# Moving part of the delta net's first head into the stage before it, in a two-layer network on one core

## What is computed

```python
x = x + latent_cross_attention(norm(x), ctx)    # 16 heads, rotary
x = x + attention(norm(x))                      # 16 heads of 16, scores multiplied by a triangle
x = x + hadamard_ffn(norm(x))                   # 256 -> 2*1024 -> 256
x = x + cross_attention(norm(x), ctx)           # 16 heads of 16, causal
x = x + gated_delta_net(norm(x))                # 32 value heads of 128, 16 key heads of 128
x = x + mixture_of_experts(norm(x))             # 32 experts of 96, the best 8
```

```python
q, k, v = silu(conv4(h @ Wqkv.T))               # a causal convolution of 4 taps along the tokens
g = -exp(A_log) * softplus(h @ Wa.T + dt_bias);  beta = sigmoid(h @ Wb.T)
# per token:  state = state * exp(g);  delta = (v - k @ state) * beta
#             state = state + outer(k, delta);  out = q @ state
o = out * rsqrt(mean(out**2)) * norm_w * silu(h @ Wz.T);   y = o @ W_out.T
```

## Time and profile before

| | us |
|---|---|
| median of 3 executions | 1669.58 (1667.72 to 1670.84) |
| the profiled execution, its own time | 1666.14 |
| its span, from first to last instruction | 1664.3 |
| PE busy in the span | 1547.2 (93%) |
| DVE busy | 1130.2 (68%) |
| ACT, POOL busy | 598.3 (36%), 553.9 (33%) |

### The profile page before, as it was taken

The page is one execution under the profiler, slowest core; times in us unless marked ns, Lnnn a source line. Parts: engine busy times, 40 slices in busy tenths (PEclk is TensorE's granted clock), DMA queues, the critical chain, the costliest instruction groups (busy, mean ns, idle before and its releaser), DMA issues. The chain is left out here.

```text
span 1664.3 us, 34006 instructions
## 1 busy us (share of the span) xinstructions
PE 1547.2 (93%) x14224; PEld 1084.9 (65%) x14224; DVE 1130.2 (68%) x1745; ACT 598.3 (36%) x1038; POOL 553.9 (33%) x885
## 2 busy tenths in 40 slices
PE   7999679979996698999999999999999996999999
PEld 3444358867883366777777777767777784565556
DVE  4666487597675677788888888887788833543433
ACT  2223144345333334444444444444544531111110
POOL 1200052123211545556545465454564431000000
PEclk9999889989998799999999999999999997999999
DMA  7533300010000121121121221112211113200000
GB/s 217 159 90 91 76 1 1 25 28 1 1 1 7 30 42 35 42 56 47 37 52 42 47 50 48 37 46 43 55 46 34 43 27 151 84 1 0 13 1 13
DMA packets 150536, 75.76 MB, mean 46 GB/s; under 512 B 128304, under 2 KB 131632, under 8 KB 148592
## 3 DMA queue, kind: packets, MB, share of 16 engines
q1 hardware_dynamic: 150384, 73.60, 17.5%
HBM read 55.73 MB, written 17.83 MB: 44 GB/s over the span
## 5 line engine op out<-in xcount | busy, mean ns | idle before, releaser
L1719 DVE SCALAR_TENSOR_TENSOR acc<-PS,wc,acc 128x504 f32<-128x504 f32 (+2 forms) x384 | 281.4, 733 | 93.2 <-ACT acc L1452 84.1
L2004 PE MATMUL PS<-HT,wgu 128*128 128x512 f32 x384 | 173.8, 597 | 0.6 <-ACT HT L2050 0.6
L1452 ACT ACTIVATE acc<-PS,wc 128x512 f32<-128x512 f32 x128 | 87.8, 686 | 172.3 <-PE PS L1183 119.7
L1183 PE MATMUL PS<-HT,wv 128*128 128x512 f32 x256 | 128.6, 626 | 11.4 <-DVE acc L1719 11.4
L1729 DVE SCALAR_TENSOR_TENSOR y<-th,acc 128x512 f32<-128x512 f32 x128 | 115.9, 906 | 22.7 <-ACT th L1456 21.4
L1183 PE MATMUL PS<-HT,wkq 128*128 128x512 f32 x256 | 124.5, 610 | 6.6 <-DVE acc L1719 4.7
L1642 POOL TENSOR_TENSOR rr<-nm,con 128x16 f32<-128x16 f32 x16 | 46.8, 2927 | 241.1 <-DVE nm L1747 241.1
L1200 PE MATMUL PS<-wz,HT 128*128 128x256 f32 x512 | 125.1, 392 | 0.7 <-DMA wz<-in_gdn_w 0.7
L2004 PEld LDWEIGHTS PS<-HT,wgu 128*128 128x128 f32 x384 | 73.3, 192 | 74.8 <-issue 72.7
L2140 DVE SCALAR_TENSOR_TENSOR act<-th,PS 128x512 f32<-128x512 f32 x48 | 33.0, 687 | 127.2 <-ACT th L2064 127.2
L1346 PE MATMUL PS<-wo,ogT 128*128 128x256 f32 x512 | 115.3, 383 | 3.5 <-DVE dl L1782 2.4
(11 more groups left out here) (252 smaller groups left out, 3036.5 us busy)
## 6 DMA issues: line engine op xcount, KB each, us to landing
a_rows<-AT SPq DMA_DIRECT2D x16, 512.0 KB, 2.6
wk<-in_l0x_k SPq DMA_DIRECT2D x16, 384.0 KB, 3.6
wgu<-in_moe_gu SPq DMA_DIRECT2D x6, 1024.0 KB, 14.9
queries_scratch<-tts SPq DMA_DIRECT2D x32, 128.0 KB, 2.7
wkq<-in_gdn_w SPq DMA_DIRECT2D x16, 256.0 KB, 2.7
wv<-in_gdn_w SPq DMA_DIRECT2D x16, 256.0 KB, 2.7
wz<-in_gdn_w SPq DMA_DIRECT2D x16, 256.0 KB, 3.3
wo<-in_gdn_w SPq DMA_DIRECT2D x16, 256.0 KB, 3.0
```

The lines of the kernel that those rows point to most:

```text
L1183: mm = pe.matmul(PS[:, QB[q], :], w[:, o:o + DK], HT[:, k, f * 512:(f + 1) * 512], start=(k == 0), stop=(k == DC - 1))
L1452: a.activation(acc[:, f, :], PS[:, QB[q], :], ACT.Copy, scale=wc[:, h % 2, 4 * c + 3:4 * c + 4]).then_inc(s["tap"], 1)
L1719: v.scalar_tensor_tensor(a0, p0, wc[:, h % 2, 4 * c + 2 - k:4 * c + 3 - k], a0, ALU.mult, ALU.add).then_inc(s["conv"], 1)
L2004: mm = pe.matmul(PS[:, 2 * (i % 2) + w, :], wgu[:, m, k, w, :], HT[:, k, f * N:(f + 1) * N], start=(k == 0), stop=(k == DC - 1))
```

## The change

Four parts; all arithmetic on the values stays, but for its order.

1. *Stage two.* The four lists are written anew: the same units in another order, and new ones at the end, `w_project`, `w_tap`, `w_conv`, `w_tanh`, `w_silu` (units 0, 2 and 4 of head 0, all on tiles 0 to 3) and `w_ab` (the decay projections of tiles 0 to 6). Their buffers acc, th and half of y (yA) now lie over kvT and W2, which stage two has done with; yB is the other half.
2. *Start of stage three.* The order of head 0's other units is 1, 3, 5, 6, 7 (PLACE numbers them behind the three done). `project_ab` has one tile left and comes first; part of the elementwise work goes from DVE to POOL. All four z projections of head 0 stand ahead of `cross(0, 4)`, in banks 5 and 7. POOL does `substitute(1)` ahead of `clear(0)`.
3. *Every head.* `factors` takes the power of the k half first, and of the q half behind Et.
4. *End of stage three.* The mean square is taken ahead of the two `gate`s; the last scaling is split over POOL (first value head) and DVE (second), as are the two copies; the layer norm of tiles 0 to 3 is done between the two last residuals; the first four packs of expert weights (wg0) are loaded behind `blocks_in(0)`.

```diff
@@ stage two: starts of PE's and DVE's lists
-                turn_x(0, 0); turn_x(0, 1); context(0); turn_x(1, 0); out_x(0); score_x(2, 1); turn_x(1, 1); score_x(3, 1)
-                context(1); turn_x(2, 0); out_x(1); turn(0, 0); turn_x(2, 1); project(0, 0); context(2); turn(1, 0)
+                turn_x(0, 0); turn_x(1, 0); turn_x(0, 1); turn_x(1, 1); context(0); context(1); out_x(0); out_x(1)
+                score_x(2, 1); score_x(3, 1); turn_x(2, 0); turn(0, 0); project(0, 0); turn(1, 0); turn_x(2, 1); turn_x(3, 0)
...
-                spread_x(1, 0); spread_x(0, 0); sums_x(1, 0); sums_x(0, 0); spread_x(0, 1); butterfly(0); sums_x(0, 1)
-                butterfly(1); spread_x(1, 1); butterfly(2); sums_x(1, 1); spread_x(2, 0); residual(0, 0); spread_x(3, 0)
+                spread_x(1, 0); spread_x(0, 0); sums_x(1, 0); sums_x(0, 0); spread_x(0, 1); spread_x(1, 1); sums_x(0, 1)
+                sums_x(1, 1); butterfly(0); butterfly(1); butterfly(2); spread_x(2, 0); spread_x(3, 0); residual(0, 0)
@@ stage two: ends of the lists of PE, ACT and DVE
+                project(5, 1); down(6); down(7); scores(5, 1); turn(6, 2); turn_p(4, 1); project(6, 1); values(4, 1)
+                turn(7, 2); scores(6, 1); project(7, 1); project_out(4, 1); turn_p(5, 1); scores(7, 1); values(5, 1)
+                project_out(5, 1); turn_p(6, 1); values(6, 1); turn(4, 3); project_out(6, 1); w_project(0); turn(5, 3)
+                w_project(1); turn_p(7, 1); w_project(2); values(7, 1); turn(6, 3); project_out(7, 1); w_ab(); turn(7, 3)
...
+                keep_o(6, 1); keep_hT(4, 3); w_tap(0); keep_hT(5, 3); w_tap(1); keep_p(7, 1); w_tanh(0); keep_o(7, 1)
+                w_tanh(1); keep_hT(6, 3); w_tap(2); w_tanh(2); keep_hT(7, 3)
...
+                stats(5, 3); sums(7, 1); apply(5, 3); residual(6, 3); stats(6, 3); w_conv(0); apply(6, 3); w_conv(1)
+                w_silu(0); w_silu(1); residual(7, 3); w_conv(2); stats(7, 3); w_silu(2); apply(7, 3)
@@ stage two: the new units
+                def w_project(k):
+                    if k == 0:
+                        pe.wait_ge(s["hT0"], 8)
+                    elif k == 2:
+                        pe.wait_ge(s["w_conv"], 3)
+                    w = wk if k < 2 else wv
+                    for c in range(DC):
+                        o = c * 2 * DK + (k % 2) * DK
+                        mm = pe.matmul(PS[:, k % 2, :], w[:, o:o + DK], HT[:, c, 0:512], start=(c == 0), stop=(c == DC - 1))
+                    mm.then_inc(s["w_pj"], 1)
+                def w_ab():
+                    for p in range(3):
+                        pe.wait_ge(s[f"hT{p}"], 8)
+                    for n in range(TILES - 1):
...
+                def w_conv(k):
+                    for i in range(3):
...
+                        v.scalar_tensor_tensor(a0, p0, wc[:, 0, 4 * k + 2 - i:4 * k + 3 - i], a0, ALU.mult, ALU.add).then_inc(s["w_conv"], 1)
+                def w_silu(k):
+                    v.wait_ge(s["w_th"], k + 1)
+                    v.scalar_tensor_tensor(yA[:, k, :], th[:, k % 2, :], 1.0, acc[:, k % 2, :], ALU.add, ALU.mult).then_inc(s["w_y"], 1)
@@ stage three: PE
-                project(0, 0)
                 project(0, 1)
-                project_ab()
-                for q in range(2, 5):
-                    project(0, q)
+                project(0, 3)
+                project(0, 5)
+                decay_sums(0)
                 scores(0)
-                decay_sums(0)
-                for q in range(5, NQ):
-                    project(0, q)
+                project(0, 6)
+                project_z(0, 0)
+                project(0, 7)
+                project_z(0, 1)
                 turn_v(0, 0)
+                def first():
+                    project(1, 0)
+                    turn_v(0, 1)
+                    project(1, 1)
+                    project_z(0, 2)
+                    decay_sums(1)
+                    project(1, 2)
+                    project_z(0, 3)
+                    project(1, 3)
+                    project(1, 4)
+                    cross(0, 4)
+                    scores(1)
+                    grow(0, 4)
+                    project(1, 5)
...
@@ stage three: POOL
-                    g.tensor_tensor(rr[:, par, :], nm[:, :], C("mhalf")[:, 0:2 * TILES], ALU.pow).then_inc(s["rr"], 1)
+                    kh, qh = slice(0, TILES), slice(TILES, 2 * TILES)
+                    g.tensor_tensor(rr[:, par, kh], nm[:, kh], C("mhalf")[:, kh], ALU.pow).then_inc(s["rr"], 1)
...
+                    g.tensor_tensor(rr[:, par, qh], nm[:, qh], C("mhalf")[:, qh], ALU.pow).then_inc(s["rr"], 1)
@@ stage three: DVE at the end
+                    level(j)
+                    for hv in range(2):
+                        gate(hv)
+                    v.wait_ge(s["fz"], j * 2 + 2)
+                    v.wait_ge(s["gz"], j * 2 + 2)
+                    v.tensor_tensor(dl[:, 1, :, :], dl[:, 1, :, :], each(ms[:, 1, :], DK), ALU.mult).then_inc(s["og1"], 1)
                     residual(g, 1)
...
+                keep_second_out()
                 residual(LAST, 0)
+                v.wait_ge(s["xa"], LAST * 2 + 1)
+                for t in range(4):
+                    stats(t)
...
                 residual(LAST, 1)
+                v.wait_ge(s["nrt"], 1)
+                for t in range(4):
+                    v.tensor_scalar(hn[:, t, :], X[:, t, :], mv[:, t, 0:1], rstd[:, t, :], ALU.subtract, ALU.mult)
@@ stage three: SP
                 blocks_in(0)
+                sp.dma_start(wg0[:, :, :, :, :], d["moe_gu"][:, 0:PIECE, :, :, :]).then_inc(s["gin"], 16)
```

More of the change, by code:

```diff
@@ L26 @@
 SUB = 16
+PIECE = 4
 BIG = 1e30
@@ new lines, in _ @@
+                score_x(4, 0); turn(2, 2); project(2, 1); up_gate(3, 1); turn_p(1, 1); score_x(4, 1); scores(2, 1)
+                values(1, 1); down(3); project_out(1, 1); turn_x(4, 0); turn(1, 3); score_x(5, 0); turn(3, 2); project(3, 1)
+                turn_p(2, 1); score_x(5, 1); turn_x(4, 1); scores(3, 1); values(2, 1); context(4); project_out(2, 1)
+                out_x(4); turn_x(5, 0); turn_p(3, 1); turn(2, 3); values(3, 1); score_x(6, 0); project_out(3, 1)
+                turn_x(5, 1); turn(4, 0); score_x(6, 1); context(5); project(4, 0); out_x(5); scores(4, 0); turn_x(6, 0)
@@ new lines, in _ @@
+                turn(3, 3); turn_x(6, 1); score_x(7, 0); context(6); turn(5, 0); score_x(7, 1); project(5, 0); turn_p(4, 0)
+                out_x(6); turn_x(7, 0); values(4, 0); scores(5, 0); turn_x(7, 1); turn(6, 0); project_out(4, 0); context(7)
+                project(6, 0); out_x(7); turn(4, 1); turn_p(5, 0); scores(6, 0); hadamard(4); values(5, 0); up_gate(4, 0)
+                turn(7, 0); project_out(5, 0); project(7, 0); up_gate(4, 1); turn(5, 1); scores(7, 0); turn_p(6, 0)
+                hadamard(5); down(4); up_gate(5, 0); values(6, 0); turn_p(7, 0); project_out(6, 0); up_gate(5, 1)
@@ L1433, in last @@
                     project_out(g, 3)
-                for j in range(LAST):
+                first()
+                for j in range(1, LAST):
                     step(j)
@@ L1866, in _ @@
+                conv(0, 5)
                 norms(0)
[L1867 to L1868 removed]
+                silu(0, 5)
+                conv(0, 6)
                 for hv in range(2):
                     make_A(0, hv)
+                silu(0, 6)
                 for hv in range(2):
                     make_P(0, hv)
[L1873 to L1876 removed]
+                silu_z(0, 0)
@@ new lines, in _, with first @@
+                conv(0, 7)
+                silu_z(0, 1)
+                silu(0, 7)
+                def first():
+                    conv(1, 0)
+                    conv(1, 1)
+                    silu(1, 0)
+                    silu_z(0, 2)
+                    conv(1, 2)
+                    silu(1, 1)
+                    silu_z(0, 3)
+                    conv(1, 3)
+                    silu(1, 2)
+                    silu(1, 3)
+                    conv(1, 4)
+                    norms(1)
+                    update(0, 4)
+                    silu(1, 4)
+                    conv(1, 5)
+                    silu(1, 5)
+                    make_A(1, 0)
+                    make_A(1, 1)
+                    update(0, 5)
+                    conv(1, 6)
+                    silu(1, 6)
+                    make_P(1, 0)
+                    make_P(1, 1)
+                    for hv in range(2):
+                        keep_M(0, hv)
+                    conv(1, 7)
+                    silu(1, 7)
+                    gates(0, False)
```

497 lines of the change are left out of this document (291 added, 206 removed).

## The result

The changed kernel takes 1656.73 us (median of 15 executions, 1648.14 to 1666.60) against 1669.11 (15 executions of the kernel before, 1665.18 to 1672.15). The ratio is 0.9927, 95% interval 0.9911 to 0.9943: 12.4 us faster, where 26 were forecast. The profiled execution took 1657.85 us, its span is 1656.1, so 8.2 us less than the span before. The two differences don't contradict each other: the profiled execution of before was 3.0 us faster than its median, that of after 1.1 slower than its own.

The account below looks back on a forecast made before the run. The prediction took PE to bound the kernel, with gains only inside stage two and at stage three's ends. Terms 1 to 4, -19 + 5 - 8 - 4 = -26, took 1669.6 to 1643.6 us; own range 1632 to 1652, wider 1630 to 1657.

Parts of the forecast that it names:

- Term 3: Inside stage two: the new order of units cuts PE's starving and low clock, -8 us, bounds -14 and +4.
- The sums: Stage two: PE and DVE unit times added in both orders; PE loses 2.3 less at the start, 3.9 in the middle.
- the last bound: Stage two, Term 3's bound of +4: the sums see no waits between units, and pairs expose each engine to delay.
- At no cost: the split power of the later heads: Later heads of stage three: two more POOL instructions, A 1.2 us earlier, no PE wait there to lose; no time change.
- Term 1: Start of stage three: A of head 1 and all behind it come earlier, taken as -19 us, bounds -10 and -24.
- my one named risk: Start of stage three: wg0's 1 MB load behind blocks_in(0) might delay A's loads, 2 us.
- Term 2: End of stage two: the units moved there add +5 us, bounds +1 and +10.
- Term 4: Passage into stage four: first gate_up at 1401.5 instead of 1405.59, -4 us, bounds -6 and -1.
- The port rule: Stage three's tail: DVE and POOL reading SBUF block each other fully, so both scalings run in turn; 1.2 us less gain.
- The moved units win nothing: Start of stage three: DVE, not T, sets PE's start; 1661 us, chance 0.05.
- The slower rival: Stage two: the new order's pairs let one late unit hold two tiles; +30, 1674 us, chance 0.06.
- the first rival: Start of stage three: A's chain keeps most of its length, A moves by 7 rather than 13; 1654 us, chance 0.13.

Follow-up runs that it names:

- order_only: The kernel before with only stage two's four lists in the new order, no new units: 1670.01 us, ratio 0.9993.
- old_order: The changed kernel with stage two's four lists back in the old order, new units kept at the tail: 1660.88 us, ratio 0.9944.
- w2: The changed kernel with eight unread products, four ahead of turn(1, 3) and four ahead of turn_p(3, 1) in stage two: 1650.43 us, ratio 0.9881.
- w3b: The changed kernel with 5, 7, 3 and 3 unread products in PE's waits at stage three's start: 1649.63 us, ratio 0.9876.
- sk_first: The changed kernel with POOL making sk right behind the k half's power, ahead of Ed, in every head: 1655.56 us, ratio 0.9920.
- clear_first: The changed kernel with POOL's clear(0) ahead of substitute(1) again: 1657.94 us, ratio 0.9925.
- wg0_later: The changed kernel with the 1 MB load wg0 behind step 2 of SP's list instead of behind blocks_in(0): 1657.51 us, ratio 0.9936.
- z_back: The changed kernel with head 0's four z units back behind the first T, by the later heads' step function: 1663.14 us, ratio 0.9964.
- best: The changed kernel with the edits of sk_first, w2, w3b and wends_b, and keep_out(15, 0) ahead of scale_wo(15) on ACT: 1647.66 us, ratio 0.9850.
- fill_mid: The changed kernel with sk ahead of Ed and the unread products of w2 and w3b only, none at the stages' ends: 1650.14 us, ratio 0.9878.
- wends_b: The changed kernel with 6, 2, 7, 3 and 4 unread products at the ends of stages two and three: 1655.27 us, ratio 0.9904.

## Why the prediction was right and wrong

The direction held. The size was off by more than half, in two steps. That the range of 1630 to 1657 held the time, 1656.73, is luck: it did so by 0.3 us, the changed kernel measured once more gave 1658.87, and the forecast's own range, 1632 to 1652, missed both.

- **Term 3, the order of stage two: -8 forecast, +0.8 measured (-1 to -2.6 by `order_only` and `old_order`).** This step failed, twice over. *The sums*: PE's idle time was to fall by 2.3 + 3.9 = 6.2 us and fell by 2.6. Up to 340 us it went from 10.0 to 9.5: PE's waits for POOL's division fell from 5.5 to 3.9 us and those for ACT from 3.5 to 2.2, but those for DVE grew from 0.8 to 2.8. Waits from unit to unit are what such sums don't see (the last bound named them and was put at an end). In the middle, from 340 to 400, it went from 8.6 to 6.5, where the sums had 11.0 and 7.1 for the middle: they were some 2 us too high for the kernel before already, where its trace could be read beside them. *The clock*: I took 2 us of gain for it, since less idle time should mean less low time. In both profiles of the changed kernel it was more: one wait of 4.8 us became two of 1.9 and 1.8, and low time in the middle rose from 10 to 17 us, a loss of 3.4. `w2` shows that it lies behind these two waits: with them filled it is gone. It doesn't follow each time (`order_only`, `w3b`), so 3.4 us is what these profiles show and no fixed price.
- **"At no cost: the split power of the later heads": 0 forecast, +4.8 measured.** I asked what A gains, and not what the power of the q half, moved behind Et, makes late: sk, which stood ahead of Ed before, stood behind it now, though it needs the k half alone, and ACT waits for sk ahead of `tanh_z`. The earlier trace rows showed that PE had no slack. `sk_first` shows the cause of the 14 waits for z, 4.8 us in all, and takes them away. It isn't a cure for the stretch as a whole, which stayed 5 us above the kernel before with half of low time taken off (724.5 against 719.5); what holds it there in place of z, the wait for Xs first of all, stays open.
- **Term 1: -19 forecast, -15.5 measured.** The mechanism was right and the milestones too: `scores(0)` 12.9 (11.9 forecast), A of head 0 24.4 (24.5), `cross(0, 4)` 51.8 (51.3), A of head 1 69.1 (68), `turn_v(1, 0)` over at 83.2 (80), the power on 8 columns 1.64 (1.65). Missing are 3.0 us between A of head 1 and `turn_out(0, 0)`, 27.6 instead of 24.6: 1.0 of clear(0), foreseen (though `clear_first` shows that the old place costs as much), and 2.0 for a_rows landing in 4.6 us instead of 2.6. `wg0_later` rules out my one named risk. In `z_back`, `best` and `fill_mid` it lands in 2.7 again; why, stays open. Another 1.1 is low clock behind `turn_out`.
- **Term 2: +5 forecast, +3.5 measured**; w_conv lies between the last residuals as placed. With the old order (`old_order`) it was +6. The 8.9 us of DVE in its working are 8.7 by its own figures.
- **Term 4: -4 forecast, -3.2 measured.** `project_out(15, 0)` starts 27.2 us behind `cross(15, 5)`, as forecast, but takes 8.86 us for being half at the low clock, where `wends_b` needs 7.1. The port rule weighed there holds: POOL's scaling took 2.93 us beside DVE's and 1.90 alone. The 1.2 us that were put on it weren't lost: `turn_out` began at 1378.42 without waiting, right behind `project_out(14, 2)` and `project_out(14, 3)`, which the low clock had stretched to 5.31 us.
- **Rivals.** None came about as written. "The moved units win nothing" gave 1661 with term 3 at -3, but PE waits for T at `cross(0, 4)`, so its mechanism is false. The slower rival put 30 us on pairs of units in stage two, which as a whole grew by 4.0 with the moved units in it. By its own figures the first rival, term 1 at -10, gives 1652.6 and not 1654.

## What to carry to other kernels

A wait of PE costs its length and at times the low clock behind it, which can be more: count waits, not only idle time, and test with a few unread products in the wait whether the clock is the price. Size such a fill from a measured product (0.86 us here), since one that runs over its wait delays what stands behind it. When an instruction is moved behind another, list the readers of everything that moves with it. Before a sum of two engines' work is used for a new order, compare it with the idle time that the trace of the old one has; here 2.6 of 6.2 us came. And read a gain in the stretch that was edited as well as in the median: in `w2` and `w3b` the median moved by twice as much as the stretch.

## What the hardware showed unexpectedly

- Behind two waits of PE, 1.86 us and then 0.56 within 2 us, some 10 us ran at 1.2 GHz (windows at 350 to 365 of the changed kernel), and behind the same two waits in `order_only` none.
- Of the 18 us between the fastest and the slowest execution of one kernel all but 5 were the clock's.
- DVE and POOL scaling 128x1024 side by side, both from SBUF: DVE 1.23 us as for other operations of this shape, POOL 2.93 instead of 1.90. The Trainium skill, "SBUF — State Buffer", SBUF: two separate sides, has the loser of the shared port pair wait for the whole of the other's instruction; the trace agrees, with 1.03 us of delay for 1.23.
- POOL's power costs 0.54 us on one column, 1.01 on 4, 1.64 on 8 and 2.91 on 16: nearly in a straight line.
